# One core, a mixture of experts: the next tile's rows are transposed inside half 0, and their two parts are made ahead of that half's relu

## The chip, the cores and the metric

The kernel runs on one core of a Trainium2 chip. A core has five engines that work side by side and meet only at semaphores: TensorE (PE in the profile; its weight loads are PEld), VectorE (DVE), ScalarE (ACT), GpSimd (POOL) and SyncE (SP). The metric is the device time of one execution in microseconds. Three runs of the kernel before gave 558.37 us in the median (557.31 to 559.39).

## The reference, cut to what matters

```python
h = layernorm(x) ; h = (h - mean over time) * rsqrt(var over time) * gamma[subject] + beta[subject]
h_flat = h.reshape(-1, 256)                          # 4096 tokens
probs = softmax(h_flat @ router_w)                   # 8 experts
gates, idx = top_k(probs, 2); gates = gates / gates.sum(-1)
hid  = relu(h_flat @ exp_w1[e] + exp_b1[e])          # 256 -> 1024
eout = hid @ exp_w2[e] + exp_b2[e]                   # 1024 -> 256
out  = x + sum over the 2 chosen experts of gate * eout
```

Each token goes through its two chosen experts only. The matrix products are in fp32 accuracy: each operand is split into a high and a low part of 16 bits, and three products stand for one.

## The kernel before

The first part (until about 122 us) normalises x, works out the router, and sorts the pairs of token and expert into 71 tiles of 128 slots, each tile of one expert. The second part runs the 71 tiles; one turn of its loop is called a step here, and step t is written out in four programs, one for each engine. The order inside each program is the order of the code; nothing is scheduled by a tool. The names are these.

- TensorE, `step` (lines 716 to 726). `products(0, t)` makes the first half of tile t's hidden layer (4 groups of 128 hidden columns, 6 matmuls each, line 691), and interleaved with each group 3 matmuls (line 698) of the second layer of tile t-2. Then `tile_transpose(t+1)` (line 657) transposes the 128 gathered rows of the next tile in two fp32 matmuls into PSUM bank 4. Then `slot_table(t+3)` (line 647) makes, in two matmuls, the table from which VectorE works out which tokens are in tile t+3. Then `products(1, t)` makes the second half of tile t, interleaved with the second layer of tile t-1.
- ScalarE, `step` (540 to 546). `relu(t, 0)` (four ACTIVATE, line 524), `tile_hi(t+1)` (line 531: the high part of the transposed rows), `gate_y(t-2)` (line 538), `relu(t, 1)`.
- VectorE, `step` (1051 to 1077). `gate(t)` (line 1000), `bias_y(t-2)` (1020), `slot_steps(t+4)` (968), `split_hi(t, 0)` (1010), `tokens_compare(t+3)` (976, 977), `split_lo(t, 0)` (1015), `tile_lo(t+1)` (1004: the low part), `tokens_count` (982), `split_hi(t, 1)`, `tokens_place` (986, 987), `split_lo(t, 1)`, `tokens_index(t+3)` (995, 996; writes `idxg` and `tok`, the row numbers of tile t+3).
- GpSimd. `gather(t)` (line 390) fetches the 128 rows of tile t from `h_rows` in DRAM by an indirect DMA. It waits for `tokens_index(t)` and, as there are two row buffers, for `gate(t-2)`, the last reader of its buffer. `scatter(t)` (line 401) adds the results to the output. Both come from one queue in turn.

`products(0, t)` waits for `tile_lo(t)` (line 666). `tile_transpose(t)` waits for the gather of tile t. The kernel before lets `slot_table(t)` wait for VectorE only in its first four calls (line 642).

Each engine also reads the experts' numbers of coming tiles into its registers (line 207, a TENSOR_LOAD, not counted as busy): VectorE and ScalarE ahead of every fourth step, TensorE ahead of every eighth.

Of the kernel before, what the change touches and what calls it, by code (L numbers as in the profile page):

```python
# [35 lines left out]
TILES = (2 * N + E * (P - 1)) // P  # L36
# [15 lines left out]
def moe_kernel(nc, x, ids, ln_g, ln_b, subj_emb, hyp_w1, hyp_b1, hyp_w2, hyp_b2, sty_w1, sty_b1,  # L52
# [13 lines left out]
    with ExitStack() as ctx:  # L66
# [359 lines left out]
        def _(act):  # L426
# [92 lines left out]
            def relu(t, par, half, b1_t):  # L519


                act.wait_ge(s_hm, 2 * t + half + 1)
                for c in range(4 * half, 4 * half + 4):
                    ins = nc.scalar.activation(hid32[:, par, c * P:(c + 1) * P], bk_hid[half][:, (c - 4 * half) * P:(c - 4 * half + 1) * P],  # L524
                                               ACT.Relu, bias=vcol[:, bass.ds(b1_t * FC + c, 1)], scale=1.0 / WSCALE)
                ins.then_inc(s_relu, 1)

            def tile_hi(t, par):

                act.wait_ge(s_gt, t + 1)  # L530
                nc.scalar.activation(hThi[:, par, :], bk_g[:, 0:D], ACT.Copy).then_inc(s_hi, 1)  # L531
# [6 lines left out]
                nc.scalar.activation(yout[:, par, :], ysum[:, par, :], ACT.Copy, scale=gates[:, bass.ds(t, 1)]).then_inc(s_yo, 1)  # L538

            def step(t, par, e):  # L540
                relu(t, par, 0, e)
                if not (isinstance(t, int) and t + 1 == TILES):
                    tile_hi(t + 1, 1 - par)
                if not (isinstance(t, int) and t < 2):
                    gate_y(t - 2, par)
                relu(t, par, 1, e)
# [11 lines left out]
        def _(pe):  # L558
# [79 lines left out]
            def slot_table(t, par):  # L638

                if isinstance(t, int) and t < 4:
                    pe.wait_ge(s_step, t + 1)
                    if t > 0:
                        pe.wait_ge(s_tok, t)
                for h in range(NH):
                    ins = nc.tensor.matmul(bk_tab[:, 0:P + 2], step16[:, par, h, :], table[:, h, :], start=(h == 0), stop=(h == NH - 1))  # L647
                ins.then_inc(s_tab, 1)

            def tile_transpose(t, par):  # L650
                if isinstance(t, int):
                    pe.wait_ge(s_gh[par], 16 * (t // 2 + 1))
                else:
                    pe.wait_ge(s_gh[par], (t - par) * 8 + 16)

                for k in range(KD):
                    ins = nc.tensor.transpose(bk_g[:, k * P:(k + 1) * P], hg[:, par, k * P:(k + 1) * P], ident)  # L657
                ins.then_inc(s_gt, 1)

            def products(half, t, par, e, ty, par_y, e_y):  # L660

                yhalf = 1 - half
                if t is not None and half == 0:
                    pe.wait_ge(s_lo, t + 1)
                if ty is not None:
                    pe.wait_ge(s_split, 2 * ty + yhalf + 1)
                if t is not None and t > 0:

                    pe.wait_ge(s_relu, 2 * t + half - 1)
                for i in range(4):
                    lhs, rhs = {}, {}
                    if t is not None:
                        c = 4 * half + i
                        lhs = {(w, k): weights(w_bytes[w], e, k * FF + c * P, P) for w in range(2) for k in range(KD)}
                    if ty is not None:
                        c = 4 * yhalf + i
                        rhs = {w: weights(w_bytes[w], e_y, UNIT + c * D, D) for w in range(2)}

                    for a in lhs.values():
                        pe.lower_ap(a, for_matmul_weights=True)
                    for a in rhs.values():
                        pe.lower_ap(a)
                    if t is not None:
                        o = bk_hid[half][:, i * P:(i + 1) * P]
                        n = 0
                        for w, parts in ((0, (hThi, hTlo)), (1, (hThi,))):
                            for k in range(KD):
                                for h in parts:  # L690
                                    hid_ins = nc.tensor.matmul(o, lhs[w, k], h[:, par, k * P:(k + 1) * P], start=(n == 0), stop=(n == 3 * KD - 1))  # L691
                                    n += 1
                    if ty is not None:
                        c = 4 * yhalf + i
                        n = 3 * c
                        for h, ws in ((hidhi, (0, 1)), (hidlo, (0,))):
                            for w in ws:
                                y_ins = nc.tensor.matmul(bk_y[par_y][:, 0:D], h[:, par_y, c * P:(c + 1) * P], rhs[w],  # L698
                                                         start=(n == 0), stop=(n == 3 * FC - 1))
                                n += 1  # L700
                if t is not None:
                    hid_ins.then_inc(s_hm, 1)
                if ty is not None:
                    y_ins.then_inc(s_ym, 1)
# [11 lines left out]
            def step(t, par, es):  # L716

                def tile(u):
                    return None if isinstance(u, int) and not 0 <= u < TILES else u

                products(0, tile(t), par, es[2], tile(t - 2), par, es[0])
                if tile(t + 1) is not None:
                    tile_transpose(t + 1, 1 - par)
                if tile(t + 3) is not None:
                    slot_table(t + 3, 1 - par)
                products(1, tile(t), par, es[2], tile(t - 1), 1 - par, es[1])
# [12 lines left out]
        def _(ve):  # L739
# [311 lines left out]
            def step(t, par, at, e, e_y):  # L1051
                def tile(u):
                    return not isinstance(u, int) or 0 <= u < TILES

                other, tokens = 1 - par, tile(t + 3)
                gate(t, par, e)
                if tile(t - 2):
                    bias_y(t - 2, par, e_y)
                if tile(t + 4):
                    slot_steps(t + 4, par)  # L1060
                split_hi(t, par, 0)
                if tokens:
                    tokens_compare(t + 3, other)
                split_lo(par, 0, at + 1)
                if tile(t + 1):
                    tile_lo(t + 1, other)
                n = 1
                if tokens:
                    tokens_count(other, at + 3)
                    n = 4  # L1070
                split_hi(t, par, 1)
                if tokens:
                    tokens_place(other, at + 4)
                split_lo(par, 1, at + n + 1)
                if tokens:
                    tokens_index(t + 3, other, at + 6)
                return 6 if tokens else 2
# [55 lines left out]
```

## Time and profile before

| what | value |
|---|---|
| median of three runs | 558.37 us |
| the profiled execution's own time | 561.23 us |
| its span in the trace | 559.5 us |
| busy: PE / DVE / POOL / ACT | 473.8 / 402.1 / 293.4 / 291.3 us |
| steps in the second part | 71 |

The profile is of one execution. Starts are microseconds from the start of the span. The chain of waits goes back from the last instruction to whatever released each step; "issue" in it is time in which the engine waited for nothing that the profile shows. Matmuls overlap one another, so the chain credits each with the time until the next one's end; a matmul's own row starts about 0.16 us ahead of its piece in the chain.

### The profile page before, as it was taken

What the parts mean: (1) busy time and instruction counts of PE and PEld (TensorE: products, weight loads), DVE (VectorE), ACT (ScalarE), POOL (GpSimd) and SP (SyncE); (2) the same over time, 40 slices, a digit from 0 to 9 for tenths busy, and PEclk for the clock granted to TensorE, in tenths of its full rate; (3) what the DMA queues carried; (4) which work ended last, traced back from release to release, by engine and by line L of the source; (5) the groups of instructions that cost most, each with busy time, mean ns of one, the idle gap of its engine ahead of it and who ended that gap; (6) DMA issues with size and microseconds to landing.
All of it is one profiled execution on the core that took longest, in us unless ns stands there. A gap on an engine that the chain in (4) does not pass through costs nothing.

```text
span 559.5 us, 16211 instructions
## 1 busy us (share of the span) xinstructions
PE 473.8 (85%) x5671; PEld 433.5 (77%) x5671; DVE 402.1 (72%) x1488; ACT 291.3 (52%) x819; POOL 293.4 (52%) x426
## 2 busy tenths in 40 slices
PE   2366465707999999999999999999999999999990
PEld 1266465606998998989999899898998989999990
DVE  3789878897676777777767777777677776777750
ACT  3878767703455455554555445544554455554540
POOL 4031312545555565665666656556656566665642
PEclk9999999999999999999999999999999999999996
DMA  8999995141222322223222232232322322323221
GB/s 266 354 317 333 310 321 191 43 127 30 37 45 49 50 48 46 46 51 49 48 45 48 50 50 46 45 49 48 47 45 50 50 40 50 50 50 50 40 40 19
DMA packets 36417, 51.36 MB, mean 92 GB/s; under 512 B 7804, under 2 KB 29718, under 8 KB 36214
## 3 DMA queue, kind: packets, MB, share of 16 engines
q0 software_dynamic: 16128, 27.59, 25.0%
q1 hardware_dynamic: 20214, 22.78, 12.7%
q8 instruction: 47, 0.77, 0.6%
q14 instruction: 28, 0.23, 0.1%
HBM read 32.24 MB, written 18.11 MB: 90 GB/s over the span
## 4 chain that ended last, share of the span: by engine, by line
PE 75%; DMA 8%; issue 6%; DVE 5%; POOL 3%; ACT 2%; POOLq 0%; DVEq 0%; ACTq 0%
PE bank L691 35%; PE bank L698 32%; DMA out_rows<-xs 6%; PE bank L657 3%; PE bank L586 2%; POOL hT L319 2%; PE bank L647 1%; PE bank L577 1%; POOL out_rows L401 1%; DVE xn L950 1%; DMA xs<-in_x 1%; PE bank L567 1%; DMA out_rows<-xs,idxs 1%; DVE wlo L852 1%; DMA xs<-h_rows,idxg 1%
## 5 line engine op out<-in xcount | busy, mean ns | idle before, releaser
L698 PE MATMUL bank<-whi,stage 128*128 x1136 | 276.9, 273 | 0.0
L524 ACT ACTIVATE hT<-bank,vcol 128x128 f32<-128x128 f32 x568 | 162.8, 368 | 207.5 <-PE bank L691 206.2
L691 PE MATMUL bank<-xn,whi 128*128 128x128 f16 x2272 | 219.9, 219 | 8.0 <-issue 3.9
L691 PEld LDWEIGHTS bank<-xn,whi 128*128 x2272 | 167.2, 98 | 34.3 <-issue 24.5
L691 PE MATMUL bank<-xn,wlo 128*128 128x128 f16 x1136 | 156.7, 220 | 0.0
L698 PE MATMUL bank<-wlo,stage 128*128 x568 | 154.8, 273 | 0.0
L401 POOL DMA_INDIRECT out_rows<-xs,idxs x71 | 115.5, 1627 | 20.1 <-issue 20.1
L1010 DVE CAST stage<-hT 128x512 f16<-128x512 f32 x142 | 65.6, 462 | 74.0 <-ACT hT L524 56.5
L698 PEld LDWEIGHTS bank<-whi,stage 128*128 128x128 f16 x1136 | 111.2, 98 | 6.6
L298 POOL TENSOR_TENSOR held_gp<-zero 1x1 f32<-1x1 f32 x150 | 41.4, 276 | 138.4 <-DVE tok L996 104.4
L1015 DVE TENSOR_TENSOR stage<-hT,stage 128x512 f16<-128x512 f32 x142 | 97.0, 683 | 0.2
L390 POOL DMA_INDIRECT xs<-h_rows,idxg x71 | 72.6, 1023 | 35.0 <-issue 33.3
L691 PEld LDWEIGHTS bank<-xn,wlo 128*128 x1136 | 87.7, 98 | 0.0
L698 PEld LDWEIGHTS bank<-wlo,stage 128*128 128x128 f16 x568 | 55.6, 98 | 0.1
L1020 DVE SCALAR_TENSOR_TENSOR xn<-bank,hrow 128x256 f32<-128x256 f32 x71 | 30.1, 424 | 33.8 <-PE bank L698 33.5
L577 PE MATMUL bank<-cst,hT 128*128 128x128 f32 x64 | 15.7, 426 | 33.0 <-POOL hT L319 31.7
L968 DVE TENSOR_SCALAR xn<-cst,stcol 128x128 f16<-128x128 f32 x142 | 43.2, 348 | 0.0
L577 PEld LDWEIGHTS bank<-cst,hT 128*128 128x128 f32 x64 | 12.7, 226 | 35.7 <-POOL hT L319 24.2
L538 ACT ACTIVATE xs<-xn,gates 128x256 f32<-128x256 f32 x71 | 37.7, 531 | 3.1 <-DVE xn L1020 3.1
L531 ACT ACTIVATE xn<-bank 128x256 f16<-128x256 f32 x71 | 28.4, 401 | 14.6 <-PE bank L657 14.6
L852 DVE SCALAR_TENSOR_TENSOR wlo<-stage,whi 128x2048 f32 (+1 forms) x14 | 32.5, 2326 | 1.1 <-ACT whi L474 0.4
L586 PEld LDWEIGHTS bank<-rw,hT 128*128 128x128 f32 x128 | 28.1, 333 | 4.1 <-POOL hT L319 4.1
(145 smaller groups left out, 509.0 us busy)
## 6 DMA issues: line engine op xcount, KB each, us to landing
stage<-in_L_cond_exp_w SPq DMA_DIRECT2D x16, 1024.0 KB, 8.2
xs<-in_x POOLq DMA_DIRECT2D x8, 512.0 KB, 5.7
out_rows<-xs POOLq DMA_DIRECT2D x8, 512.0 KB, 7.4
h_rows<-hrow SPq DMA_DIRECT2D x8, 512.0 KB, 8.7
xs<-h_rows,idxg POOLq DMA_INDIRECT x71
out_rows<-xs,idxs POOLq DMA_INDIRECT x71
hrow<-in_L_cond_exp_b SPq DMA_DIRECT2D x1, 1024.0 KB, 4.7
cst<-in_consts SPq DMA_DIRECT2D x1, 243.5 KB, 2.7
```

Source lines behind the costliest of these rows:

```text
L298: gp.tensor_tensor(held_gp[:, kind:kind + 1], zero[0:1, 0:1], zero[0:1, 0:1], ALU.add).then_inc(s_held[kind], 1)
L390: gp.indirect_dma_start(out=hg[:, par, :], out_offset=None, in_=h_dram, in_offset=bass.IndirectOffsetOnAxis(ap=idxg[par][:, 0:1], axis=0)) ...
L401: gp.indirect_dma_start(out=out, out_offset=bass.IndirectOffsetOnAxis(ap=idxs[par][:, 0:1], axis=0), in_=yout[:, par, :], in_offset=None, ...
L524: ins = nc.scalar.activation(hid32[:, par, c * P:(c + 1) * P], bk_hid[half][:, (c - 4 * half) * P:(c - 4 * half + 1) * P], ACT.Relu, bias= ...
L538: nc.scalar.activation(yout[:, par, :], ysum[:, par, :], ACT.Copy, scale=gates[:, bass.ds(t, 1)]).then_inc(s_yo, 1)
L586: ins = nc.tensor.matmul(bk_log[par][:, j * E:(j + 1) * E], hT[:, par, k * T + j * P:k * T + (j + 1) * P], rw[:, k * E:(k + 1) * E], start ...
L691: hid_ins = nc.tensor.matmul(o, lhs[w, k], h[:, par, k * P:(k + 1) * P], start=(n == 0), stop=(n == 3 * KD - 1))
L698: y_ins = nc.tensor.matmul(bk_y[par_y][:, 0:D], h[:, par_y, c * P:(c + 1) * P], rhs[w], start=(n == 0), stop=(n == 3 * FC - 1))
L852: V.scalar_tensor_tensor(out=wlo[:, bass.ds(at, UNIT)], in0=stage[:, slot, :], scalar=WSCALE, in1=whi[:, bass.ds(at, UNIT)], op0=ALU.mult, ...
L968: ins = V.tensor_scalar(step16[:, par, h, :], slotrow, stcol[:, h:h + 1], cst[:, bass.ds(t + C_NEGT, 1)], ALU.subtract, ALU.is_ge)
L1010: V.tensor_copy(hidhi[:, par, a:b], hid32[:, par, a:b]).then_inc(s_dv, 1)
L1015: V.tensor_tensor(hidlo[:, par, a:b], hid32[:, par, a:b], hidhi[:, par, a:b], ALU.subtract).then_inc(s_split, 1)
```

## The change

TensorE's two transposes of the next tile move from the end of half 0 to behind its first group of four. On ScalarE `tile_hi(t+1)` goes ahead of `relu(t, 0)`. On VectorE `tile_lo(t+1)` goes from behind `split_lo(t, 0)` to right behind `gate(t)`, so ahead of `bias_y`. `slot_table(t)` now waits in every call for `slot_steps(t)` and for `tokens_index(t-1)`. Nothing is computed that was not computed before.

```diff
@@ ScalarE @@
             def step(t, par, e):
-                relu(t, par, 0, e)
                 if not (isinstance(t, int) and t + 1 == TILES):
                     tile_hi(t + 1, 1 - par)
+                relu(t, par, 0, e)
@@ TensorE @@
-                if isinstance(t, int) and t < 4:
-                    pe.wait_ge(s_step, t + 1)
-                    if t > 0:
-                        pe.wait_ge(s_tok, t)
+                pe.wait_ge(s_step, t + 1)
+                if t > 0:
+                    pe.wait_ge(s_tok, t)
...
+                    if half == 0 and i == 0 and t is not None and t + 1 < TILES:
+
+                        tile_transpose(t + 1, 1 - par)
...
                 products(0, tile(t), par, es[2], tile(t - 2), par, es[0])
-                if tile(t + 1) is not None:
-                    tile_transpose(t + 1, 1 - par)
                 if tile(t + 3) is not None:
                     slot_table(t + 3, 1 - par)
@@ VectorE @@
                 gate(t, par, e)
+                if tile(t + 1):
+                    tile_lo(t + 1, other)
                 if tile(t - 2):
                     bias_y(t - 2, par, e_y)
...
                 split_lo(par, 0, at + 1)
-                if tile(t + 1):
-                    tile_lo(t + 1, other)
```

TensorE before, at the border of the two halves of step 4 (line 657 is the transposes of tile 5, 647 the slot table of tile 7):

```order
L698 MATMUL bank<-whi,stage 128x256
L698 MATMUL bank<-wlo,stage 128x256
L698 MATMUL bank<-whi,stage 128x256
L657 MATMUL bank<-cst,xs 128x128 [waits rows_gathered1]
L657 MATMUL bank<-cst,xs 128x128
L647 MATMUL bank<-table,xn 128x130 x2
L682 ISA [waits hidden_relu,hidden_split]
L691 MATMUL bank<-xn,whi 128x128 x4
```

TensorE in the changed kernel, the first group of step 4 and what follows (all lines of TensorE's program are one lower there: 656 is the transposes, 646 the slot table):

```order
L681 ISA [waits hidden_relu,hidden_split,tile_lo_ready]
L683 REGISTER_ALU
L690 MATMUL bank<-xn,whi 128x128 x4
L690 MATMUL bank<-xn,wlo 128x128 x2
L697 MATMUL bank<-whi,stage 128x256
L697 MATMUL bank<-wlo,stage 128x256
L697 MATMUL bank<-whi,stage 128x256
L656 MATMUL bank<-cst,xs 128x128 [waits rows_gathered1]
L656 MATMUL bank<-cst,xs 128x128
L681 ISA
L690 MATMUL bank<-xn,whi 128x128 x4
```

and further down, at the border of its halves:

```order
L697 MATMUL bank<-whi,stage 128x256
L646 MATMUL bank<-table,xn 128x130 [waits slot_tokens_ready,slot_steps_ready]
L646 MATMUL bank<-table,xn 128x130
L681 ISA [waits hidden_relu,hidden_split]
L690 MATMUL bank<-xn,whi 128x128 x4
```

So the transposes, with their wait for the gather, stand three groups earlier, and the slot table has got a wait of its own.

VectorE before, from the end of step 10 into step 11:

```order
L996 TENSOR_TENSOR tok<-rt 128x1
L1000 ISA
L1000 COPY gates<-xs 128x1
L1020 ISA [waits y_products]
L1020 SCALAR_TENSOR_TENSOR xn<-bank,hrow 128x256
L968 TENSOR_SCALAR xn<-cst,stcol 128x128 x2
L1010 CAST stage<-hT 128x512 [waits hidden_relu]
L976 TENSOR_SCALAR xn<-bank,cst 128x128 [waits slot_table_done]
L977 ISA rj,rt<-bank,cst 128x2
L977 ISA rt 128x1
L1015 TENSOR_TENSOR stage<-hT,stage 128x512 [waits vector_tile_chain]
L1004 TENSOR_TENSOR xn<-bank,xn 128x256 [waits tile_hi_ready]
```

VectorE in the changed kernel, the same place:

```order
L996 TENSOR_TENSOR tok<-rt 128x1
L1000 ISA
L1000 COPY gates<-xs 128x1
L1004 TENSOR_TENSOR xn<-bank,xn 128x256 [waits tile_hi_ready]
L1020 ISA [waits y_products]
L1020 SCALAR_TENSOR_TENSOR xn<-bank,hrow 128x256
L968 TENSOR_SCALAR xn<-cst,stcol 128x128 x2
L1010 CAST stage<-hT 128x512 [waits hidden_relu]
L976 TENSOR_SCALAR xn<-bank,cst 128x128 [waits slot_table_done]
L977 ISA rj,rt<-bank,cst 128x2
L977 ISA rt 128x1
L1015 TENSOR_TENSOR stage<-hT,stage 128x512 [waits vector_tile_chain]
```

`tile_lo` (line 1004) has moved over seven instructions that make the second layer's bias, the slot steps and half 0's split.

## Rows read from the trace of the kernel before

**Rows 1.** The profile's page: busy time, share of the span and instructions of each engine.
```profile
PE 473.8 (85%) x5671; PEld 433.5 (77%) x5671; DVE 402.1 (72%) x1488; ACT 291.3 (52%) x819; POOL 293.4 (52%) x426
```

**Rows 2.** Chain of waits, steps 30 and 31: start us, us, what.
```profile
303.26 0.06 issue
303.32 0.49 PE bank L691 x6
303.82 0.33 PE bank L698 x3
304.14 0.33 PE bank L691 x6
...
306.13 0.22 PE bank L657 x2
306.35 0.12 PE bank L647 x2
...
309.11 0.21 issue
...
315.12 0.06 issue
```

**Rows 3.** Chain of waits, first piece of step 3 and of step 68.
```profile
145.56 0.49 PE bank L691 x6
...
526.25 0.46 PE bank L691 x6
```

**Rows 4.** Timeline of step 30: start us, us, engine, line, what, [idle before <-releaser].
```profile
305.54 0.14 DVE L996 TENSOR_TENSOR tok<-rt 128x1 int32<-128x1 f32 x1
...
305.97 0.38 PE L657 MATMUL bank<-cst,xs 128*128 128x128 f32 x2
...
306.56 0.99 POOL L390 DMA_INDIRECT xs<-h_rows,idxg  x1 [0.49 <-issue]
...
308.65 0.41 DVE L1004 TENSOR_TENSOR xn<-bank,xn 128x256 f16<-128x256 f32 x1
...
309.32 0.38 PE L691 MATMUL bank<-xn,whi 128*128 128x128 f16 x4 [0.21 <-DVE xn L1004]
```

**Rows 5.** Stretches of the trace: us, busy of each engine, PEclk, DMA share, GB/s.
```profile
308.60:308.90 0.30, 0.30 (x7) 0.22 (x4) 0.30 (x2) 0.00 (x0) 0.30 (x1) 1.00 0.51 197
308.90:309.10 0.20, 0.20 (x2) 0.00 (x0) 0.20 (x2) 0.17 (x1) 0.20 (x1) 1.00 0.01 0
```

**Rows 6.** Timeline, the first gather and TensorE behind it.
```profile
122.72 1.21 POOL L390 DMA_INDIRECT xs<-h_rows,idxg  x1 [0.55 <-POOL held_gp L298]
...
125.81 0.69 PE L657 MATMUL bank<-cst,xs 128*128 128x128 f32 x2 [3.47 <-DMA xs<-h_rows,idxg]
```

**Rows 7.** Timeline of steps 31 and 32: VectorE, with a register load between the two rows, then GpSimd.
```profile
317.39 0.14 DVE L996 TENSOR_TENSOR tok<-rt 128x1 int32<-128x1 f32 x1
318.05 0.15 DVE L1000 COPY gates<-xs 128x1 f32 x1 [0.51 <-issue]
...
319.01 0.99 POOL L390 DMA_INDIRECT xs<-h_rows,idxg  x1 [0.49 <-issue]
```

**Rows 8.** Waits: engine, line, waited for: us in total, times, longest us.
```profile
POOL idxs L397 <- DMA out_rows<-xs,idxs: 10.0, 8, 2.3
```

**Rows 9.** Timeline around step 0: the wait of a slot table.
```profile
131.20 0.15 DVE L996 TENSOR_TENSOR tok<-rt 128x1 int32<-128x1 f32 x1
...
131.50 0.28 PE L647 MATMUL bank<-table,xn 128*128 128x130 f16 x2 [0.64 <-DVE tok L996]
131.63 0.40 PE L691 MATMUL bank<-xn,whi 128*128 128x128 f16 x4
```

**Rows 10.** Chain of waits where TensorE had read registers (step 64).
```profile
502.91 0.51 PE bank L691 x6
```

**Rows 11.** The first steps: GpSimd's gather of tile 2, and the chain at step 2.
```profile
133.37 0.96 POOL L390 DMA_INDIRECT xs<-h_rows,idxg  x1 [0.49 <-POOL held_gp L298]
...
139.75 0.49 PE bank L691 x6
```

## The prediction, on record before the changed kernel ran

> **What bounds the kernel now.** I read four views in this order. The page's busy times: PE is busy 473.8 of 559.5 us and every other engine much less [rows 1]; in the tile loop TensorE is almost without idle time, so only what stops it there can shorten the kernel. The chain of waits over two steps shows what is left: a group of half a layer is 0.33 us of line 691 and 0.33 us of line 698, eight of them with 0.22 us of transposes and 0.12 us of slot table fill the step, and the only irregular place is the start of half 0, where the chain has 0.06 to 0.21 us of "issue" and a first piece of 0.49 instead of 0.33 us [rows 2]. The timeline says what stands there: VectorE's `tile_lo` (line 1004) starts at 308.65, ends at 309.06, and TensorE's matmul starts at 309.32 [rows 4]. So TensorE waits at each step's start for the low part of the tile, which is late because it stands behind relu, split and slot compare of half 0. Last, the timeline of GpSimd, for what the change will ask of the gather.
>
> **What a step costs, and what its floor is.** From the first piece of step 3 to that of step 68 are 65 steps: (526.25 - 145.56) / 65 = 5.857 us each [rows 3]. Without the wait a step is the time from 303.32 to 309.11, 5.79 us, less the 0.16 us by which its first piece is too long: 5.63 us [rows 2]. If nothing else stops TensorE, 65 x (5.857 - 5.63) = 14.7 us go. (Term A: -14.7.)
>
> **Part 1: `tile_hi` and `tile_lo` earlier.** They are neither more nor longer. In the changed order the transposes end about 1 us into the step, `tile_hi` finds ScalarE between its relus, and `tile_lo` stands right behind `gate(t)`. In the rows of before the index ends at 305.68 [rows 4]; 0.07 us of gate and 0.41 us of `tile_lo` later it is 306.2, three microseconds ahead of the next half 0. `bias_y` waits for the second layer's products of half 0 until about then, so it is hardly delayed. In the steps with a register load the load puts `gate` 0.66 us later [rows 7] and all of VectorE's chain for half 0 is some 0.4 us later than before; it has that slack, since `split_hi(t, 1)` waits for ScalarE anyway. I take 0 for this part.
>
> **Part 2: the gather is needed earlier.** This is the price. Let E be the end of a half 1 in the chain, 303.26 for step 30 [rows 2]. Tile 32 is transposed in step 31; in the changed kernel its transposes want to start one step and one group later than E: E + 5.63 + 0.66 - 0.16 = E + 6.13 (0.16 is the distance between a matmul's row, 305.97, and its piece, 306.13 [rows 2, 4]). For tile 32 that is 309.39. The gather itself hangs on `tokens_index`, which hangs on relu and split of the half 1 that ended at E, so it does not move with the transposes. It is issued at 306.56 and GpSimd is done with it at 307.55 [rows 4]. When has it landed? No row names it for this tile; the nearest two bound it. Its packets still run in 308.60 to 308.90 and are gone by 308.90, 1.35 us behind GpSimd's end [rows 5]. At the start TensorE stood waiting for the first gather: GpSimd's end at 123.93, the transposes at 125.81, 1.88 us behind [rows 6]. I take 1.65, between them: 309.20. An ordinary gather so lands 0.19 us before it is wanted, and costs nothing.
>
> Not so in every fourth tile. VectorE reads its registers between `tokens_index` and `gate`, and the gather waits for `gate`, which frees its buffer. In step 32 this makes 318.05 of what else were 317.46; the gather of tile 34 is done on GpSimd at 320.00 [rows 7] and lands at 321.65. E is 315.12 there [rows 2], the transposes want to start at 321.25, so TensorE stands 0.40 us. There are 17 such tiles: 17 x 0.40 = 6.8 us. (Term B: +6.8.) With 1.35 us it would be 0.10 us each, 1.7 in all; with 1.88 us 0.63 each, 10.7, and the ordinary 48 would each be 0.04 late, 1.9. Besides, single DMAs are late: 8 of the 71 scatters were waited for, 10.0 us in all [rows 8]. If five gathers are as late as to cost 0.35 each, an estimate, that is 1.7. (Term C: +1.7; 0 to 3.)
>
> *A rule beside this row.* For a gather the rows give 309.20 - 306.56 = 2.64 us from issue to landing by my choice, 2.34 to 2.87 by the bounds. The Trainium skill, "DMA: Bandwidth & Descriptors", section "Anatomy of one DMA — SWDGE (gpsimd) path", fits a fixed 2.0 us and bytes / 436e3 to this kind of DMA; for 128 rows of 1056 bytes that is 2.31 us, an estimate from the page, just under my lower bound. By it the gathers would cost next to nothing (the second rival below).
>
> **Part 3: the slot table's new wait.** It waits for `tok` of the tile before, which ends at 305.68 [rows 4]. Its own turn comes at E + 8 x 0.33 + 0.22 - 0.16 = E + 2.70 = 305.96 in the changed kernel. From the end of `tok` to the table's matmul TensorE took 0.15 us where it did stand waiting (131.35 to 131.50), and to the following half's first matmul 0.28 us [rows 9]. So the table could start at 305.83 and half 1 at 305.96 against a turn at 306.07. Both margins are 0.1 us; a later `tok` of single steps eats them. Below nothing this can't be; if `tok` came 0.3 us later in all steps it would be 0.2 each. I take 0.02 on the mean of 65 steps, nearest to the row. (Term D: +1.1.) *A rule beside this row.* The Trainium skill, "TensorE: Matmul & The Clock Gate", section "Architectural detail: the array is 16× 32×32, not 1× 128×128", gives TensorE's queue 64 places. By it a wait that ends before the queue has run dry costs nothing, and D would be 0 rather than 1.1; no row here shows the queue's length.
>
> **Part 4: small ones.** TensorE reads its registers ahead of every eighth step. Before, the wait covers it; where `tile_lo` came early enough, in step 64, the first piece was still 0.51 us [rows 10], 0.17 over a whole one. Eight times: +1.4 (term E). At the start, step 1 could begin earlier, but its transposes now want tile 2, whose gather is done on GpSimd at 134.33 [rows 11], landing about 136.0. Behind it stand 0.22 of transposes, three groups without second layer (1.0), the table (0.12) and half 1 (2.65): step 2 starts at 140.0 to 140.1 instead of 139.75 [rows 11], and step 3 about 0.2 later too (term F: +0.2).
>
> **The sum.** -14.7 + 6.8 + 1.7 + 1.1 + 1.4 + 0.2 = -3.5 us. The profiled execution's own time is 561.23 us with a span of 559.5; it becomes 557.7. The median of before lies 2.9 us under that execution, at 558.37, so I forecast **554.9 us** for the median.
>
> **The rivals.**
>
> *The gathers land in time.* If the landing is 1.35 us behind GpSimd's end, term B is 1.7 and C 0.0: -14.7 + 1.7 + 1.1 + 1.4 + 0.2 = -10.3, 548.1 us. For it: the packets are all gone by then [rows 5]. Against it: the one time that TensorE was seen to wait it took 1.88 us [rows 6]. Chance 0.13.
>
> *The gathers are late in all steps.* With 1.88 us: -14.7 + 10.7 + 1.9 + 2.0 + 1.1 + 1.4 + 0.2 = +2.6, 561.0 us. The wait for the gather has then taken the place of the wait for the low part. For it: [rows 6]; against: that was the first gather, with 1.21 us on GpSimd instead of 0.99. Chance 0.20.
>
> *The slot table's wait decides, slower.* The place is the border of the halves in every step, the wait for `tok`. It decides from the point where `tok` ends more than 0.1 us later after E than the 2.42 us of now. At 0.3 us later each step loses 0.2: 65 x 0.2 = 13.0 in place of 1.1, while a longer step gives the gathers more time (17 x 0.2 and part of C, 4.2 back): -3.5 + 11.9 - 4.2 = +4.2, 562.6 us. For it: VectorE's chain is tight, and it now has `bias_y` and all that follows later in the steps with a register load. Against: `tok` hangs on the relu of half 1, for which VectorE waits. Chance 0.08.
>
> *The change doesn't do what it says.* The gap at the step's start is TensorE's own (registers, refilling) and stays: 558.4 us. Against: the matmul follows the end of `tile_lo` by 0.26 us [rows 4], and half 1, with the same kind of waits, has no such gap [rows 2]. Chance 0.06.
>
> **How the numbers follow.** The forecast has 0.53, with a range of its own of 552.5 to 557.5. What a measurement of this kernel can tell from no change is about 0.5%, 2.8 us: faster is below 555.6. The forecast lies just past this border, so 0.6 of its chance is faster and the rest the same: faster 0.53 x 0.62 + 0.13 = 0.46; same 0.20 + 0.19 + 0.06 = 0.45; slower 0.09. The range of 8 in 10 reaches from 549.0, which leaves out half of the second case, to 561.0, which takes in the gathers being late and leaves out the slower one.
>
> **What would show it.** TensorE's wait for line 1004 gone from the chain; the step at 5.63 us in three of four steps and about 6.0 in those where tile t+1 was gathered behind a register load; the new idle time of TensorE in front of the transposes, put down to the DMA of `xs<-h_rows,idxg`, 8 us or so in all; next to nothing in front of the slot table. The forecast is wrong if ordinary steps wait for the gather or for `tok`, or if no step waits for the gather.

## The result, and the profile after

The changed kernel is slower by half a per cent: ratio 1.0051 to the kernel before, interval 1.0033 to 1.0070. The medians of 20 runs each are 561.67 us (558.06 to 569.50) after and 558.01 us (556.80 to 560.39) before; the ratio leaves out runs more than 1.5% above the fastest of their kernel, which are six of after's (567.30 to 569.50), so it stands for some 560.9 us. The forecast was 554.9. The profiled execution of after took 560.21 us with a span of 558.5, and comes from the lower end of its runs. The 20 runs of after spread over 11.4 us, those of before over 3.6; that is part of the result.

The page of after: busy time as in [rows 1]; the chain that ended last by engine and by line; and the group of the transposes.

```profile
PE 475.2 (85%) x5671; PEld 438.4 (78%) x5671; DVE 401.5 (72%) x1488; ACT 297.7 (53%) x819; POOL 286.8 (51%) x426
...
PE 50%; DMA 18%; DVE 12%; issue 9%; ACT 5%; POOL 3%; ACTq 1%; DVEq 0%; POOLq 0%
PE bank L690 22%; PE bank L697 20%; DMA xs<-h_rows,idxg 12%; DMA out_rows<-xs,idxs 4%; PE bank L656 3%; ACT hT L524 3%; PE bank L586 2%; DVE stage L1010 2%; DMA out_rows<-xs 1%; PE bank L567 1%; DVE stage L1015 1%; PE bank L577 1%; PE bank L646 1%; DVE tns L781 1%; ACT whi L474 1%
...
L656 PE MATMUL bank<-cst,xs 128*128 128x128 f32 x142 | 29.8, 292 | 13.2 <-DMA xs<-h_rows,idxg 12.2
```

TensorE's work is the same. What is new is the gather's DMA with 12% of the chain, where all DMAs together had 8% in before. (These 12% are not lost time: once TensorE has waited for a gather, the chain is charged with the whole flight, such as the 3.58 us below.) The waits of after say the same (what waited, for whom: us in total, times, longest):

```profile
PEld bank L656 <- DMA xs<-h_rows,idxg: 22.3, 33, 3.7
PE bank L656 <- DMA xs<-h_rows,idxg: 12.2, 22, 3.4
PEld bank L690 <- issue: 3.5, 9, 1.2
PE bank L646 <- DVE tok L996: 1.5, 1, 1.5
PE bank L690 <- DVE xn L1004: 1.0, 1, 1.0
```

(6.1 of the 12.2 us are at tiles 0, 1, 2 and 70. The view counts idle time from the modelled end of the matmul before; the 12.0 us worked out below for the 65 steps alone are counted from starts, and are another sum.)

In before, the weight loads in front of the first half's groups carried the wait for the low part, and only one tile's transposes, the first, waited for a gather:

```profile
PEld bank L691 <- issue: 24.5, 69, 1.9
...
PE bank L657 <- DMA xs<-h_rows,idxg: 3.5, 1, 3.5
```

So the wait forecast to go has gone (24.5 us in 69 places have become 3.5 in 9), and the wait forecast to come has come (22.3 us in 33 places, by the weight loads as well). The same stretch as [rows 2], in after's chain (start us, us, what):

```profile
298.30 3.58 DMA xs<-h_rows,idxg
301.88 0.04 issue
301.92 0.44 PE bank L656 x2
302.36 0.34 PE bank L690 x6
...
304.35 0.12 PE bank L646 x2
304.46 0.34 PE bank L690 x6
...
307.77 0.22 PE bank L656 x2
...
312.75 0.51 PE bank L690 x6
...
313.58 0.03 issue
313.61 0.44 PE bank L656 x2
...
319.52 0.44 PE bank L656 x2
```

A transposes' piece of 0.44 instead of 0.22 us marks a wait for the gather. Tile 32 (307.77) is an ordinary tile that did not wait, tile 34 (319.52) one that was gathered behind a register load, as forecast. But tiles 31 (301.92) and 33 (313.61) are ordinary ones, and waited all the same. The slot table and half 1 follow one another without a gap. The timelines of GpSimd and TensorE show the gathers of tiles 31, 32, 33 and 34, and the transposes of the four (start us, us):

```profile
298.30 0.99 POOL L390 DMA_INDIRECT xs<-h_rows,idxg  x1 [0.49 <-issue]
...
304.34 0.99 POOL L390 DMA_INDIRECT xs<-h_rows,idxg  x1 [0.49 <-issue]
...
310.32 1.00 POOL L390 DMA_INDIRECT xs<-h_rows,idxg  x1 [0.49 <-issue]
...
316.63 0.99 POOL L390 DMA_INDIRECT xs<-h_rows,idxg  x1 [0.49 <-issue]
```

```profile
301.92 0.44 PE L656 MATMUL bank<-cst,xs 128*128 128x128 f32 x2
...
307.61 0.38 PE L656 MATMUL bank<-cst,xs 128*128 128x128 f32 x2
...
313.61 0.44 PE L656 MATMUL bank<-cst,xs 128*128 128x128 f32 x2
...
319.52 0.44 PE L656 MATMUL bank<-cst,xs 128*128 128x128 f32 x2
```

From GpSimd's end to the transposes it is 2.63 us for tile 31, 2.29 for tile 33, and 1.90 for tile 34. Over all tiles gathered behind a register load ("load tiles" from here on) that waited, this last figure is narrow, 1.83 to 1.94: it is the price of a gather that nothing disturbs, the upper bound of [rows 6] and not the 1.65 taken. The landing itself comes at 1.7 to 1.9, and TensorE 0.04 to 0.05 us behind it. The traces of before and after don't show this well: of the 16 records that tell of a gather's landing they hold well under half (463 and 430 of 1,104 for tiles 0 to 68), so that the last one held is mostly too early, and the median comes out as 1.65 and 1.67. Over the 307 gathers of all twelve traces that have their 16 records and no fetch of TensorE's program in the 1.5 us behind GpSimd's end (these fetches come below) the median is 1.82. Nor do the packets' ends tell the landing, as [rows 5] was read: these gathers land 0.30 us or more behind the end of their last packet.

Where the time went, in the 65 steps from tile 3's to tile 68's transposes. They take 381.49 us in after and 380.71 in before (142.39 to 523.10, the same length as [rows 3] gives):

```profile
137.81 0.38 PE L656 MATMUL bank<-cst,xs 128*128 128x128 f32 x2
...
519.30 0.38 PE L656 MATMUL bank<-cst,xs 128*128 128x128 f32 x2
```

Worked out from the starts of TensorE's matmuls, the time above the floor of 5.636 us a step is 14.4 us in before, nearly all of it at the step's start, and 15.2 us in after: 6.2 in front of the transposes of load tiles, 5.7 in front of those of 15 ordinary tiles, 1.4 at TensorE's register loads, and 1.9 in pieces of some 0.06 us where it takes up again behind a wait.

### The profile page after: what moved, and what is told of

Same layout as the page of the kernel before. It is cut to its first block, busy times and chain, and to the rows that moved or that the text cites. A ratio compares the mean times of both kernels' runs of the same rounds, so it can differ in the third digit from the quotient of the medians.

```text
span 558.5 us, 16278 instructions
## 1 busy us (share of the span) xinstructions
PE 475.2 (85%) x5671; PEld 438.4 (78%) x5671; DVE 401.5 (72%) x1488; ACT 297.7 (53%) x819; POOL 286.8 (51%) x426
## 3 DMA queue, kind: packets, MB, share of 16 engines
q1 hardware_dynamic: 20214, 22.78, 12.4%
## 4 chain that ended last, share of the span: by engine, by line
PE 50%; DMA 18%; DVE 12%; issue 9%; ACT 5%; POOL 3%; ACTq 1%; DVEq 0%; POOLq 0%
PE bank L690 22%; PE bank L697 20%; DMA xs<-h_rows,idxg 12%; DMA out_rows<-xs,idxs 4%; PE bank L656 3%; ACT hT L524 3%; PE bank L586 2%; DVE stage L1010 2%; DMA out_rows<-xs 1%; PE bank L567 1%; DVE stage L1015 1%; PE bank L577 1%; PE bank L646 1%; DVE tns L781 1%; ACT whi L474 1%
## 5 line engine op out<-in xcount | busy, mean ns | idle before, releaser
L690 PEld LDWEIGHTS bank<-xn,whi 128*128 x2272 | 172.8, 99 | 13.8 <-issue 3.5
L401 POOL DMA_INDIRECT out_rows<-xs,idxs x71 | 120.9, 1703 | 23.8 <-issue 23.8
L1010 DVE CAST stage<-hT 128x512 f16<-128x512 f32 x142 | 67.0, 472 | 82.9 <-ACT hT L524 68.9
L298 POOL TENSOR_TENSOR held_gp<-zero 1x1 f32<-1x1 f32 x150 | 31.8, 212 | 140.1 <-DVE tok L996 105.6
L390 POOL DMA_INDIRECT xs<-h_rows,idxg x71 | 70.8, 998 | 35.0 <-issue 33.3
L531 ACT ACTIVATE xn<-bank 128x256 f16<-128x256 f32 x71 | 27.2, 383 | 33.7 <-PE bank L656 32.3
L656 PE MATMUL bank<-cst,xs 128*128 128x128 f32 x142 | 29.8, 292 | 13.2 <-DMA xs<-h_rows,idxg 12.2
L656 PEld LDWEIGHTS bank<-cst,xs 128*128 128x128 f32 x142 | 15.9, 143 | 23.6 <-DMA xs<-h_rows,idxg 22.3
```

What stands on the lines that cost most here:

```text
L298: gp.tensor_tensor(held_gp[:, kind:kind + 1], zero[0:1, 0:1], zero[0:1, 0:1], ALU.add).then_inc(s_held[kind], 1)
L390: gp.indirect_dma_start(out=hg[:, par, :], out_offset=None, in_=h_dram, in_offset=bass.IndirectOffsetOnAxis(ap=idxg[par][:, 0:1], axis=0)) ...
L401: gp.indirect_dma_start(out=out, out_offset=bass.IndirectOffsetOnAxis(ap=idxs[par][:, 0:1], axis=0), in_=yout[:, par, :], in_offset=None, ...
L1010: V.tensor_copy(hidhi[:, par, a:b], hid32[:, par, a:b]).then_inc(s_dv, 1)
```

## The experiments

Ten kernels, each against the kernel before on the same chip (557.93 us for the first four below; 558.61 for transposes_early_only and last_and_registers; 558.70 for the other four). The theory: moving the low part ahead is what gains, and the transposes' place is what loses, since it leaves the gather a margin near nothing. The rivals: the slot table's new wait costs the time; the early transposes cost nothing and the floor is higher than I thought.

**The transposes one and two groups later.** The margin of the gather grows by 0.66 us with each group.

```diff
-                    if half == 0 and i == 0 and t is not None and t + 1 < TILES:
+                    if half == 0 and i == 1 and t is not None and t + 1 < TILES:
```

(and `i == 2` in the second one.)

> The changed kernel with the two transposes behind the second group of half 0 instead of the first (0.66 us later in the step). Theory (the changed kernel loses at the transposes, which reach TensorE before the gathered rows have landed): in the changed kernel's tile loop, steps 3 to 67, TensorE stood 12.0 us in front of the transposes, 6.2 in steps whose gather follows a register load and 5.8 in 15 others. A turn 0.66 us later clears the first kind and leaves 1 to 2 us of the second, so against the kernel before about -14.4 (its waits for the low part) + 1.6 (TensorE's register loads) + 1.5 + some 1.5 in the first steps = -9.8: 547 to 549 us. Rival (the reordering on ScalarE and VectorE, or the slot table's new wait, is what costs): no change against the changed kernel, 560 to 562 us.

> The transposes behind the third group of half 0 (1.33 us later than in the changed kernel). Theory (late gathers): no wait for a gather is left in the steady steps, about -14.4 + 1.6 + up to 1 in the first steps: 545 to 547 us. Rival (reordering or the slot table's wait costs): 560 to 562 us.

Behind group 2, just above the expectation: 549.72 us, ratio 0.9865 (0.9835 to 0.9895); the 65 steps take 370.39 us. Behind group 3: 546.64 us, ratio 0.9800 (0.9772 to 0.9828); 369.50 us. Its waits, behind group 2:

```profile
PE bank L656 <- DMA xs<-h_rows,idxg: 6.7, 4, 3.4
```

The 22 waits of after have become 4: those of tiles 0 and 2 in the first steps, one of 0.58 us in the 65 steps, and tile 70's. Behind group 3 only the first two are left (5.6 us). A place 0.66 us later takes 11.1 us off the 65 steps.

**The transposes at the end of half 0, where they were; ScalarE, VectorE and the slot table's waits as changed.**

```diff
-                    if half == 0 and i == 0 and t is not None and t + 1 < TILES:
-                        tile_transpose(t + 1, 1 - par)
...
                 products(0, tile(t), par, es[2], tile(t - 2), par, es[0])
+                if tile(t + 1) is not None:
+                    tile_transpose(t + 1, 1 - par)
```

> The change on ScalarE and VectorE alone: TensorE's transposes stay at the end of half 0, as in the kernel before. tile_hi then stands ahead of relu of half 0 but its transposes come after that half, so relu and all of VectorE's chain for half 0 start about 0.6 us later. Theory: VectorE has about 1 us of slack there, the low part is still ready some 2 us before it is wanted, no gather is late: 545 to 547 us. Rival (the order of ScalarE and VectorE costs): over 558 us.

544.77 us, ratio 0.9759 (0.9728 to 0.9790). Slightly faster than expected. The 65 steps take 368.28 us, 1.9 above the floor, 1.4 of them at TensorE's register loads. Its chain, at the border of step 31's halves and at the start of step 32:

```profile
303.26 0.22 PE bank L656 x2
303.48 0.12 PE bank L646 x2
303.60 0.33 PE bank L690 x6
...
306.25 0.50 PE bank L690 x6
306.75 0.33 PE bank L697 x3
```

There is no "issue" left at the step's start; the one longer piece (0.50) is TensorE's register load, term E. The whole gain of term A is here: 380.71 - 368.28 = 12.4 us net, and 14.4 with the 1.4 of the register loads and 0.6 of refilling added back.

**The slot table's waits alone.** The kernel before with the two waits in every call.

```diff
-                if isinstance(t, int) and t < 4:
-                    pe.wait_ge(s_step, t + 1)
-                    if t > 0:
-                        pe.wait_ge(s_tok, t)
+                pe.wait_ge(s_step, t + 1)
+                if t > 0:
+                    pe.wait_ge(s_tok, t)
```

> The kernel before, with nothing of the change but the slot table's two waits in every call. Theory: the wait is over before TensorE gets there, 558 us as before (within 1 us). Rival (the forecast's slower rival, the slot table's wait as the bound): some us slower, 560 to 563.

557.57 us, ratio 0.9992 (0.9979 to 1.0006). The rival falls where this wait is concerned: it is free here, and in after nothing over 0.03 us stands in front of the table in any of the 65 steps.

**TensorE's part alone.** ScalarE and VectorE as before, the transposes behind group 1, the slot table with its waits.

```diff
             def step(t, par, e):
+                relu(t, par, 0, e)
                 if not (isinstance(t, int) and t + 1 == TILES):
                     tile_hi(t + 1, 1 - par)
-                relu(t, par, 0, e)
...
                 gate(t, par, e)
-                if tile(t + 1):
-                    tile_lo(t + 1, other)
...
                 split_lo(par, 0, at + 1)
+                if tile(t + 1):
+                    tile_lo(t + 1, other)
```

> The change on TensorE alone (transposes behind the first group, the slot table's waits); ScalarE and VectorE in the order of the kernel before. Theory: the low part still hangs on relu and split of half 0, and the transposes now stand in half 0's way instead of behind it, so relu starts 0.22 us later after the step's start and the low part too, while the step no longer has the transposes behind half 0 to wait by. A step was 5.857 us from start to low part to start and becomes 6.08: 65 x 0.22 = 14 us more, 570 to 573 us, with TensorE waiting for line 1004 in nearly every step and hardly for a gather. Rival (only the gathers matter): like the changed kernel or a little slower, 560 to 565 us.

Just under the expectation: 569.60 us, ratio 1.021 (1.019 to 1.023); 391.79 us for the 65 steps, 6.03 each. Its waits, and the start of step 30 in its chain:

```profile
PEld bank L690 <- issue: 36.3, 71, 1.9
...
PE bank L656 <- DMA xs<-h_rows,idxg: 4.2, 2, 3.5
```

```profile
304.27 0.19 issue
304.45 0.50 PE bank L690 x6
304.95 0.33 PE bank L697 x3
305.28 0.27 PE bank L656 x2
```

This is the costly half of the change in a pure form. The transposes' 0.22 us now stand ahead of groups 2 to 4 of half 0, so relu, split and, behind them, the low part come 0.2 us later (`tile_lo` starts 5.34 us behind the step's first matmul in the median, against 5.15 in before, and the next step follows its end by 0.26 in both): 0.17 us a step times 65 is 11.1 us. In the 65 steps the gather is hardly waited for, since each step is 0.4 us longer than the floor and leaves it that much more time. The two parts alone give -2.4% and +2.1%; together they give +0.5%.

**VectorE's register load out of the gather's way.** As after, but the load stands ahead of `split_hi(t, 1)`, so `gate` and the gather are no longer behind it.

```diff
+                nxt = experts(ve, t + 1) if (t + 1) % 4 == 0 and t + 1 < TILES else None
                 split_hi(t, par, 1)
...
-                if t % 4 == 0:
-                    es = experts(ve, t)
-                at += step(t, t % 2, at, es[2 + t % 4], es[t % 4])
+                n_at, nxt = step(t, t % 2, at, es[2 + t % 4], es[t % 4])
+                at += n_at
+                if nxt is not None:
+                    es = nxt
```

> The changed kernel with VectorE's register load of every fourth step moved from behind tokens_index to ahead of split_hi of half 1, where VectorE waits for ScalarE. Theory: the gather of every fourth tile is issued 0.65 us earlier and no longer waits; 6.2 us of waits at the transposes in 16 steps go, as well as their refilling: 555 us (554 to 556.5), 0.99 of the changed kernel. If the load, 1.06 us long, delays split_hi, some of it comes back as a later tok. Rival (in the steps with a register load something else than the gate holds the transposes): no change.

550.50 us (550.01 to 558.33), ratio 0.9840 (0.9806 to 0.9874): some 4 us less than expected. The load tiles' waits fell from 6.2 to 0.9 us, as they should. The other tiles' fell too, from 5.7 to 4.0, which the theory did not ask for. Its waits:

```profile
PEld bank L656 <- DMA xs<-h_rows,idxg: 13.4, 22, 3.8
...
PE bank L656 <- DMA xs<-h_rows,idxg: 6.9, 8, 3.5
```

So term B is real and rightly placed. But the 1.7 us at the ordinary tiles I can't put down to it. Nor the other 1.7 outside the 65 steps (the span is 9.2 us shorter, the 65 steps 7.5): they lie in the first three steps, whose code is the same in both, with 18.3 us instead of 20.1. There the clock fell in after's execution and not in this one (term F below).

**The first steps.** In steps 0 and 1 alone the transposes stand behind group 4.

```diff
-                    if half == 0 and i == 0 and t is not None and t + 1 < TILES:
+                    if half == 0 and i == (3 if t is not None and t < 2 else 0) and t is not None and t + 1 < TILES:
```

> The changed kernel with the transposes of steps 0 and 1 alone behind the fourth group, as before. Theory: in the changed kernel TensorE stood for the gathers of tiles 1 and 2 with most of its work still queued behind, and its clock fell to half for the following 3 us; step 3 began 20.1 us after step 0 instead of 17.9. This variant gets about 2 us back: 558.5 to 559.5 us. Rival (the start differs by chance between executions): no change, 561.

The expectation missed: 563.61 us (558.71 to 567.29), ratio 1.0105 (1.0056 to 1.0153). The beginning did what it should: from the first step's first matmul to tile 3's transposes 12.3 us instead of 15.1, and the clock stayed at 1.00. But the 65 steps gave none of it on: 381.39 us in the profiled run, with 8.7 instead of 6.2 us at load tiles and 3.1 instead of 5.7 at ordinary ones; its other three runs took 562.23 to 567.29. So the start can be mended, and the time it sets free is within the scatter of what follows. In time this experiment is inconclusive.

**Why ordinary gathers are late.** In after, 15 of the 65 gathers land over 2.0 us behind GpSimd's end (2.1 to 2.8; the other 50 at 1.5 to 1.9 by the records held). 13 of them are among the 15 ordinary tiles that made TensorE wait, with 5.0 of the 5.7 us. What marks the 15? DMA queues from 0.4 us ahead of GpSimd's end to the landing, of tile 33, then of tile 32, which landed in time (packets, MB, share of 16 engines):

```profile
q0 software_dynamic: 48, 0.14, 19.6%
q8 instruction: 1, 0.02, 2.7%
```

```profile
q0 software_dynamic: 48, 0.14, 24.7%
```

Tile 33's gather shares its time with one packet of 16 KB from the queue that brings TensorE's program (it has one for every 250 or so instructions of TensorE); for tile 31 it is one of 8 KB from the other such queue. All 15 late gathers have such a fetch beginning between 0.35 us ahead of GpSimd's end and 0.65 behind it; of the other 50 only four have. The loop has 46 fetches of 16 KB, some 8.9 us apart, of 0.9 to 1.7 us each. These limits were found on this trace; the other traces bear them out. In all twelve (before, after and the ten experiments) 205 gathers of tiles 4 to 68 landed over 2.0 us behind GpSimd's end, and 201 of them had such a fetch in progress at some time in the 1.5 us behind that end; of the 575 others 111 had. Two rivals: a fixed property of those tiles (their rows' addresses), or the phase between fetches and gathers. To shift the phase, 64 tiny matmuls (128 instructions) go ahead of TensorE's program, or 40 (80 instructions).

```diff
+            g16 = cst[:, 0:P].bitcast(F16)
+            for _ in range(64):
+                nc.tensor.matmul(bk_T[0][:, 0:E], g16[:, 0:P], g16[:, 0:E], start=True, stop=True)
```

> The changed kernel with 64 tiny matmuls (8 columns, 128 instructions with their weight loads) ahead of TensorE's first work, into a bank that is overwritten. They move every later instruction of TensorE by 128 places, and with that the moments at which its program is fetched in 16 KB pieces (46 fetches in the loop, one every 8.9 us, 0.9 to 1.5 us each on one DMA engine). Theory (the 15 late gathers of ordinary tiles are those whose DMA met such a fetch: in all 15 a fetch began between 0.35 us ahead of GpSimd's end of the gather and 0.65 us behind it): the fetches come some 4.5 us earlier in the steps, and by the trace of the changed kernel none would meet a gather; the wait at ordinary tiles falls from 5.8 us to under 1.5, the run to 555 to 557 us if the added matmuls cost nothing at the start. Rival (the late gathers are late by their addresses, or by chance): the same tiles, 8, 19, 25, 28 and so on, are late again and the time stays at 560 to 562.

> The same with 40 tiny matmuls, 80 instructions, which moves the fetches 2.8 us earlier in the steps. Theory: as many late gathers as in the changed kernel or a few fewer (about 12), but of other tiles, 13, 21, 24, 38, 41, 49, 52, 55, 57, 60 among them. Rival: the same tiles as in the changed kernel.

Both times missed by far: 571.61 us with 128 (three of four runs at 571.58 to 572.30, the fourth at 562.99), and 570.54 us (one run) with 80. There is no ratio for either, and six of after's own 20 runs took over 567 us, so in time the two decide nothing. They decide which gathers are late. With 128, 24 came late, none of them in after's list, 22 with a fetch in the 1.5 us behind GpSimd's end; with 80, 24 came late, 3 of them the same as in after. Of the kernels that don't shift the program, transposes_last and last_and_registers have all 15 of after's late tiles among their late ones, slot_waits_only has 13, t_after_group3 12, and the fewest are 4 of the 5 that were late in before. So it is not the tiles themselves, nor chance alone, though how many come late differs from trace to trace: it is the phase. But which tiles it would be I had forecast as if the timeline were rigid, and that was wrong too (with 80, one of the forecast tiles was late): each wait moves everything behind it, and the phases meet anew. The waits in front of the transposes grew from 12.0 us to 23.1 and 24.0 in the profiled executions (of 572.30 and 570.54 us). With the shift, 15 and 17 gathers met a 16 KB fetch that began 0.2 to 1.0 us behind GpSimd's end, and landed 2.5 to 3.7 us behind it; in after no 16 KB fetch began there. Why more meet than in after is left open; a kernel without the fetches was not tried, so that they cause the lateness rests on this coincidence and its moving with the phase.

**A version from what was found.** The transposes at the end of half 0 and the register load early, both edits as above.

> The kernel with the transposes last (544.8 us), with VectorE's register load moved ahead of split_hi of half 1 as well. Theory: that move gained 10 us in the changed kernel only because it took gathers off TensorE's path; here no gather is waited for, so nothing changes: 544.5 us (543.5 to 545.5). Rival (the register load costs VectorE's chain time by itself): 1 us or more faster, 543 or less.

544.09 us, ratio 0.9746 (0.9730 to 0.9762), 367.82 us for the 65 steps: the fastest measured, though not to be told from transposes_last. As the gather has its margin back, the register load's place is worth next to nothing there: half a microsecond between the two profiles' 65 steps.

## Why the prediction was wrong

The sum was -3.5 us; the ratio says +2.9 (0.0051 x 558.0). In the two profiles, from the first matmul of the loop to the end, it is 435.8 against 431.8, +4.0. (The profiled after was 1 us shorter in all only because its first part, which the change does not touch, ended 5 us earlier.) Step by step:

- **Term A, -14.7: right (14.4).** The wait for `tile_lo` is gone. In after the low part of tile 31 starts at 303.44 and is due after 307; transposes_last shows the gain by itself.
- **Term B, +6.8: right in size by luck, two errors that cancel.** 16 load tiles in the 65 steps waited 6.2 us, 0.39 each against 0.40. With 1.88 us my own working gives 0.63 each. Measured were 0.46 in the 11 load tiles whose tile before did not wait; where it had waited, that wait came off (tile 54, behind a wait of 0.65 us, had none).
- **Term C, +1.7: the step that failed.** It was mis-sized: 5.7 us. I wrote "if five gathers are as late as to cost 0.35 each". The size of each held (0.38); the number was 15. It was five in before's trace too (landings over 2.0 us), where the gather had over 2 us of margin and nobody saw them. I took their number as a property of the DMA, while it is one of the phase against the program's fetches: 15 in after, 22 in transposes_last, and 20 in slot_waits_only, whose order is that of before and whose 65 steps take the same time (380.89 us); in the last two they again cost nothing. One trace could not have told the number. The range of 0 to 3 for C should have reached to all tiles. That ordinary tiles have no margin (0.19 us by my working) was the warning, and I priced it with a mean.
- **Term D, +1.1: it measured 0.** Nothing stands in front of the slot table in after; the wait alone costs nothing (ratio 0.9992). 1.9 us of refilling stand behind the waits for the gather instead. For the table's wait the Trainium skill, "TensorE: Matmul & The Clock Gate", section "Architectural detail: the array is 16× 32×32, not 1× 128×128", would have given 0, by a queue that has not run dry; the trace agrees, with nothing over 0.03 us there in the 65 steps.
- **Term E, +1.4: right.** 1.4 in after and in transposes_last.
- **Term F, +0.2: failed, 2.2 us.** The working foresaw that step 1 would wait for tile 2's gather, but not that the clock could fall behind it. Transposes of tile 2 in the timeline, and TensorE around them (stretch, length, PE, PEld, DVE, ACT and POOL busy, granted clock, DMA share, GB/s):

```profile
131.47 0.44 PE L656 MATMUL bank<-cst,xs 128*128 128x128 f32 x2 [1.95 <-DMA xs<-h_rows,idxg]
```

```profile
129.30:131.50 2.20, 0.25 (x5) 0.08 (x2) 1.63 (x6) 1.14 (x4) 0.32 (x1) 1.00 0.22 61
131.50:133.50 2.00, 2.00 (x22) 1.99 (x23) 1.35 (x7) 0.38 (x1) 0.96 (x2) 0.66 0.00 0
133.50:135.50 2.00, 2.00 (x19) 1.82 (x17) 0.69 (x5) 1.14 (x4) 0.18 (x1) 0.50 0.25 68
135.50:137.80 2.30, 2.30 (x32) 2.17 (x30) 0.87 (x4) 0.68 (x3) 0.00 (x0) 0.99 0.00 0
```

  TensorE stood some 2 us, and then worked at 1.2 GHz (0.50) until about 135.5: 19 matmuls in 2 us where it later makes 28 (32 in 2.3). In before it had 0.60 us of work in 133.5 to 135.5 and kept 1.00. But the length of the stand alone doesn't decide it: in fetch_shift_80 TensorE stood 2.60 us in front of the same transposes, and in t_after_group3 2.11, and the clock stayed at 1.00. In fetch_shift_80 and in registers_early, where it stayed too, the first three steps took 18.3 us against 20.1 in after and 17.9 in before, so the fall cost some 1.8 of the 2.2 us in the execution that was profiled; how many of the others had it no run shows.
- **The end, not priced: 1.0 us.** The last step's transposes also moved up to their gather; there the following waits have no later step to be absorbed in.

```profile
531.09 0.44 PE L656 MATMUL bank<-cst,xs 128*128 128x128 f32 x2 [0.48 <-DMA xs<-h_rows,idxg]
```

With the measured terms the sum is -14.4 + 6.2 + 5.7 + 1.9 + 1.4 + 2.2 + 1.0 = +4.0 (A, B, C, the refilling in D's place, E, F, the end): the +4.0 between the profiles, and near the ratio's +2.9. Of the 7.5 us by which -3.5 was off, C has 4.0, F 2.0 and the end 1.0.

Of the rivals, "the gathers are late in all steps" (561.0 us) came closest in time and had the right interval (1.88), but not the right shape: 34 of the 49 ordinary tiles in the 65 steps did not wait. "The slot table's wait decides" and "the change doesn't do what it says" fall by slot_waits_only and transposes_last. "In time" falls with 22 waits. On the fixed 2.0 us and bytes / 436e3 of the Trainium skill, "DMA: Bandwidth & Descriptors", section "Anatomy of one DMA — SWDGE (gpsimd) path", the trace does not agree: by the page 2.31 us, an estimate from it; by the traces with nearly all landing records 0.99 + 1.8 = 2.8 us, and in after up to 0.99 + 2.81 = 3.8. (The prediction points at its second rival there; the one meant, that the gathers land in time, is its first.) The chance of slower was set at 0.09, since the only slower case that I made was one of a place that turned out free; a spread of the gather's landing, put in as a case with its own price, would have put a good part of the 0.20 there.

## What to carry to other kernels

Price a move of a wait by the margin that it leaves its slowest releaser, not the median one: here gathers with 0.19 us of margin by the forecast's working, and next to none by the landing at 1.8 us, lost 0.38 us in each of 15 ordinary steps, while 0.66 us more margin removed all but one. Take a change apart before it is judged: one half was worth -2.4% and the other +2.1%, and moving an operation forward inside a full engine also moves all it passes backward. Where a changed kernel's runs scatter more than those before it (here 11.4 us against 3.6), look for a wait that stands on an arrival that varies; that this made the scatter here is likely and not shown, since one execution of each kernel was traced.

## What the runs showed of the hardware

- TensorE's program comes by DMA while the kernel runs, in after in pieces of 16 KB some 8.9 us apart. The 15 late gathers, each beside a fetch, landed 2.1 to 2.8 us behind GpSimd's end; undisturbed ones land at 1.7 to 1.9. The latest in fetch_shift_128 came at 3.9. Adding 128 small instructions at the program's start changed which gathers were hit: none of after's 15, and 24 others.
- After a stand of 1.95 us in after the granted clock was 0.66 over the next 2.0 us and 0.50 over the 2.0 us behind those, though TensorE was fully busy again. After stands of 2.23 and 2.48 us at the same place (fetch_shift_128, t_after_group2) it fell as well. After 1.40 us (first_steps_late) it was still 1.00, but so it was after 2.60 us (fetch_shift_80), so the length of the stand alone does not tell. The stretches behind the two:

```profile
132.50:136.20 3.70, 3.70 (x49) 3.50 (x50) 2.54 (x9) 2.10 (x8) 1.14 (x2) 1.00 0.16 41
```

```profile
131.55 0.44 PE L659 MATMUL bank<-cst,xs 128*128 128x128 f32 x2 [2.60 <-DMA xs<-h_rows,idxg]
131.55:136.00 4.45, 4.45 (x65) 4.30 (x66) 2.50 (x9) 1.96 (x7) 1.09 (x2) 1.00 0.12 34
```

- Where TensorE stood waiting for a gather whose 16 landing records are all held, its transposes followed the last of them by 0.04 to 0.05 us (27 waits in first_steps_late). From GpSimd's end to the transposes it was 1.83 to 1.94 us in after's load tiles.
- A trace may hold well under half of the landing records of a DMA (430 of 1,104 in after, 1,086 in transposes_last), and a landing read from it is then too early: 1.67 us behind GpSimd's end in the median of after, against 1.82 for undisturbed gathers that have all their records.
